# A TensorE order: gate, up, attention step, down of three units back, in place of gate, down of four units back, up, attention step

## What is computed

```
pooled = softmax(masked scores) @ x / count      # tanh scores, mask by prompt type
x1  = x + attention(pooled)                      # 16 heads of 8, low-rank keys and values, rotary part, causal
c   = x1 @ W[category of the sequence] + b       # one of 64 matrices for each sequence
x2  = x1 + sum over 64 experts of cw[token, e] * (silu(c @ Wg[e]) * (c @ Wu[e])) @ Wd[e]
         + shared expert, silu(c @ Wsg) * (c @ Wsu) @ Wsd
cw  = 8 of 64 experts for each token, chosen out of 4 of 8 groups, weights scaled by 2.5
```

## Time and profile before

| | us |
|---|---|
| median of 3 runs | 727.07 (725.82 to 727.83) |
| the profiled execution, its own time | 730.47 |
| span of its instructions | 728.6 |
| around the span | 1.87 |
| TensorE matmul busy | 704.1 (97% of the span) |
| VectorE busy | 543.2 (75%) |
| ScalarE busy | 444.0 (61%) |
| GpSimd busy | 424.5 (58%) |
| mean granted TensorE clock | 0.988 of full speed |

### The profile page before, as it was taken

How to read it: one execution, slowest core, us unless ns; L and a number is a source line. 1 busy time by engine, 2 the same in 40 slices (tenths; PEclk the granted TensorE clock), 3 DMA queues, 4 the chain that set the end, 5 groups by cost and what they waited for, 6 DMA issues and landing times.

```text
span 728.6 us, 15761 instructions
## 1 busy us (share of the span) xinstructions
PE 704.1 (97%) x5616; PEld 547.9 (75%) x5616; DVE 543.2 (75%) x1146; ACT 444.0 (61%) x857; POOL 424.5 (58%) x351
## 2 busy tenths in 40 slices
PE   7989889999999999999999999999999999999997
PEld 5767668677887778777787778877787777888885
DVE  4787568787598676887788865986768876877664
ACT  1876755568555865468555685558654685555553
POOL 2437677665456644556455654566455664666665
PEclk8998999999999999999999999999999999999999
DMA  7333674436443553534544364444544354344451
GB/s 257 107 113 124 202 149 112 124 104 163 106 124 114 145 109 121 138 101 146 120 112 137 107 157 105 126 113 140 113 125 138 97 150 115 110 129 142 128 130 46
DMA packets 66845, 92.93 MB, mean 128 GB/s; under 512 B 7888, under 2 KB 26768, under 8 KB 66768
## 3 DMA queue, kind: packets, MB, share of 16 engines
q1 hardware_dynamic: 61728, 85.90, 43.4%
q10 hardware_dynamic: 5040, 6.03, 2.5%
HBM read 88.37 MB, written 3.15 MB: 126 GB/s over the span
## 4 chain that ended last, share of the span: by engine, by line
PE 74%; DVE 10%; ACT 5%; SPq 4%; issue 4%; DMA 2%; POOL 1%; POOLq 0%; DVEq 0%; ACTq 0%
PE banks L997 71%; DVE hid L964 3%; DVE hid L976 2%; PE banks L1077 2%; DVE k_blk L693 1%; DVE pt_sb L668 1%; SPq L302 1%; ACT banks L531 1%; SPq L296 1%; DMA x_early<-in_x_feat 1%; SPq L272 1%; ACT s_t L405 1%; ACT hid_hi L543 1%; SPq L333 1%; ACT v_blk L392 1%
## 5 line engine op out<-in xcount | busy, mean ns | idle before, releaser
L640 POOL TENSOR_TENSOR hid_lo<-hid,hid_hi 128x512 fp32r<-128x512 f32 (+1 forms) x264 | 342.1, 1296 | 261.1 <-ACT hid_hi L543 259.3
L964 DVE TENSOR_TENSOR hid<-banks,cwb 128x512 f32<-128x512 f32 x254 | 174.6, 687 | 122.1 <-ACT banks L531 115.1
L531 ACT ACTIVATE banks<-banks 128x512 f32<-128x512 f32 x254 | 147.4, 582 | 134.3 <-PE banks L997 132.7
L543 ACT CAST hid_hi<-hid 128x512 fp32r<-128x512 f32 (+1 forms) x264 | 162.7, 616 | 78.7 <-DVE hid L976 76.9
L976 DVE TENSOR_TENSOR hid<-hid,banks 128x512 f32<-128x512 f32 (+1 forms) x264 | 181.4, 687 | 25.3 <-PE banks L997 2.9
L997 PE MATMUL banks<-c_hi,wg_hi 128*128 128x512 f32 x264 | 118.9, 450 | 4.6 <-DVE hid L964 3.4
L997 PE MATMUL banks<-hid_hi,wd_hi 128*128 128x512 f32 (+1 forms) x264 | 104.6, 396 | 0.8 <-POOL hid_lo L640 0.8
L997 PE MATMUL banks<-c_hi,wg_lo 128*128 128x512 f32 x264 | 104.0, 394 | 0.0
L997 PE MATMUL banks<-c_lo,wg_hi 128*128 128x512 f32 x264 | 104.0, 394 | 0.0
L997 PE MATMUL banks<-hid_hi,wd_lo 128*128 128x512 f32 (+1 forms) x264 | 103.7, 393 | 0.0
L997 PE MATMUL banks<-hid_lo,wd_hi 128*128 128x512 f32 (+1 forms) x264 | 103.6, 393 | 0.0
(11 more groups left out here) (159 smaller groups left out, 799.0 us busy)
## 6 DMA issues: line engine op xcount, KB each, us to landing
cwb<-cw_scratch SPq DMA_DIRECT2D x254, 256.0 KB, 3.8
k_blk<-in_cond_w SPq DMA_DIRECT2D x112, 64.0 KB
xf<-in_x_feat SPq DMA_DIRECT2D x8, 256.0 KB, 3.9
out_feat<-y ACTq DMA_DIRECT2D x8, 256.0 KB, 3.4
wg_raw<-in_we_gate SPq DMA_DIRECT2D x7, 256.0 KB, 4.7
wu_raw<-in_we_up SPq DMA_DIRECT2D x7, 256.0 KB, 4.5
wd_raw<-in_we_down SPq DMA_DIRECT2D x7, 256.0 KB, 4.5
xf<-in_x_tok SPq DMA_DIRECT2D x6, 256.0 KB, 2.7
```

The lines of the kernel that those rows point to most:

```text
L531: nc.scalar.activation(dst, gate_bank(p)[:, :], ACT.Silu).then_inc(S["silu_done"], 1)
L543: nc.scalar.copy(hid_hi[0:n, slot(b, p), :], hid[0:n, slot(b, p), :]).then_inc(S["hi_ready"], 1)
L640: nc.gpsimd.tensor_sub(hid_lo[0:n, slot(b, p), :], hid[0:n, slot(b, p), :], hid_hi[0:n, slot(b, p), :].bitcast(F32)).then_inc(S["lo_ready" ...
L964: nc.vector.tensor_mul(hid[:, slot(b, p), :], gate, weight)\
```

## The change

The order of the products on TensorE within a unit is another one; nothing else is touched. Before, unit p issues G(p), D(p - 4), U(p), A(p). After, it issues G(p), U(p), A(p), D(p - 3), and three D instead of four are left after the last unit. The row buffers stay at `NH` = 4, and the code of the other engines is the same. The operations and their number are the same too.

```diff
         Y_STORED = 4
+        BEHIND = 3
         X2_MOVED = 9
...
                 three(gate_bank(p)[:, :], wg_hi[:, p, :], wg_lo[:, p, :], c_hi[par][:, :], c_lo[par][:, :], True, True)\
                     .then_inc(S["gate_done"], 1)
-                if p >= NH:
-                    down(b, p - NH)
-                elif prev:
-                    down(b - 1, UNITS + p - NH)
                 if p < NPAIR:
...
                 for step, blk in steps:
                     attention_step(step, blk)
+                if p >= BEHIND:
+                    down(b, p - BEHIND)
+                elif prev:
+                    down(b - 1, UNITS + p - BEHIND)
 
             pe.sem_inc(S["y_ready"], 1)
             pipeline(unit)
-            for p in range(UNITS - NH, UNITS):
+            for p in range(UNITS - BEHIND, UNITS):
                 down(NBLK - 1, p)
```

## The result

| | before | after |
|---|---|---|
| median, us | 727.45 (725.82 to 727.87, 4 runs) | 740.37 (740.03 to 740.68, 4 runs) |
| profiled execution, its own time | 730.47 | 740.25 |
| its span | 728.6 | 738.4 |
| mean granted clock | 0.988 | 0.991 |

The changed kernel is slower: ratio 1.0173, 95% interval [1.0158, 1.0189], +12.6 us of 727.5. The medians are 12.9 apart and the forecast said 14.7. The two profiled executions are only 9.8 us apart, because the one of before began its block 0 late: first gate product at 45.96 us against 43.24, 2.7 of the missing 3.1 us, ahead of all that the change touches.

The account below looks back on a forecast made before the run. TensorE was taken to set the pace, so reordering could mainly lose time. Stalls of 4.1 + 4.1 + 0.4 + 2.5 + 2.9 + 0.7 = 14.7 us, added to the 727.07 median, gave 741.8 us; range 733.6 to 747.7.

Parts of the forecast that it names:

- A(7), A(8): Attention steps of units 7 and 8, blocks 1 to 6: no slack, full 0.69 us slip shows, 4.1 us.
- U(0), ends of blocks 0 to 5: Next block's first up product waits for hid(32) without slack: 6 x 0.69 = 4.1 us.
- U(0), end of block 6: First up product of block 7: slack 0.35, stall 0.34 plus 0.1 for a slow first matmul, 0.4 us.
- A(3): Attention step of unit 3, blocks 1 to 6: slack 0.25 or 0.30, stalls 0.44 and 0.39, 2.5 us.
- routing: Units 17 to 26: VectorE's stretch slips, stalls 0.47 or 0.12 plus 0.1 restart per block, 2.9 us.
- the end: Last down products wait for GpSimd's chain from the last gate product, one product later: 0.7 us.
- block 0: First block: waits on loading weights in units 8 to 13 absorb the slip; zero taken, up to 0.7 us possible.
- D had room: Down products one product earlier: even at the tightest place, in routing units, 0.39 of 1.77 us left; cost nothing.
- "faster" rival: Block 0: earlier down product fills a pause, keeping the clock from falling at 96 to 104 us; 724.7 us, chance 0.05.
- All hidden: Whole kernel: shorter waits before VectorE and ScalarE than shown take up the slip; 727 us, chance 0.08.
- part hidden: Only the unit 7/8 attention and block-end first up-product terms hold, 8.2 us: 735.3 us, chance 0.14.
- clock rival: Blocks 1 to 6: new pauses bring one low-clock stretch each, 10 us added; 752 us, chance 0.05.

Follow-up runs that it names:

- experiments 5 and 6: Kernel before, with gate products of only some units moved behind the down product (5; 28; 2; 17, 18; then 17-25; 28-32; 17-27): 730.06 to 732.64 us.
- experiment 3: Changed kernel with the gate product put back ahead of the down product in units 2, 4, 5, 17, 18 and 28: 727.11 us, ratio 0.9991.
- experiment 2: Kernel before with the attention step issued ahead of the up product in each unit: 751.21 us, ratio 1.0318.

## Why the prediction was right

The forecast, 741.8, is 1.4 us above the result (14.7 us added, 12.9 found), and its mechanism held at every place of blocks 1 to 7. By the starts of TensorE's matmuls (distance before and after; blocks 1, 3, 5, then 2, 4, 6):

| term of the sum | forecast | distances | measured |
|---|---|---|---|
| A(7), A(8) | 4.1 | A(7) 0.23 to 0.86 and 0.73; A(8) 0.64 unchanged, 0.49 to 0.63 | 6 x 0.63 or 0.64 = 3.8 |
| U(0), ends of blocks 0 to 5 | 4.1 | 0.43 to 1.13, 0.62 to 1.35 | 6 x 0.7 = 4.2 |
| U(0), end of block 6 | 0.4 | 0.23 to 0.42, and 0.33 for 0.23 behind it | 0.3 |
| A(3) | 2.5 | 0.32 to 0.75, 0.33 to 0.72 | 2.5 |
| routing | 2.9 | U(17) to U(28) +0.40, +0.21 | 1.8 |
| the end | 0.7 | U(31) to the end of the last matmul 6.27 to 7.09 | 0.8 |
| block 0 | 0 | first gate to that of block 1, with the slip | -0.9 |

The rows add up to 12.5 us. The two traces are 12.5 apart as well, counted from the first gate product to the end (9.8 by the spans and the 2.7 by which before began later), and the medians 12.9. (The last row: block 0 is 102.10 us long by its gates, 102.34 before. The next block's gate has slipped by 0.69, so by U and A block 0 is 0.93 shorter. This is no effect of the order that a run could show, see below; without it 13.4 of 14.7 us were found.) Of the 0.8 at the end 0.16 is the clock's: it was granted at 0.51 over the last 3.7 us, and the last matmul of all took 0.55 in place of 0.39.

*Right.* D had room: in blocks 1 to 7 no D but the last ones waits for its row. (In block 7 D(32) starts 0.32 behind U(2) and its next matmul 0.33 behind it, which looks like a pause. But its row is ready 2.50 us earlier, at 664.15 + 2.67 = 666.82 (the second of the two operations in that line), and the kernel before has the same two distances at its D(32): it is a product with 64 rows behind one with 128.) The first two lines are the kernel before, the others the changed one:

```profile
660.73 0.39 PE L997 MATMUL banks<-c_lo,wg_hi 128*128 128x512 f32 x1
661.04 0.49 PE L997 MATMUL banks<-hid_hi,wd_hi 64*128 64x512 f32 x1
...
664.15 2.67 POOL L641 TENSOR_TENSOR hid_lo<-hid,hid_hi 128x512 fp32r<-128x512 f32 x2 [0.80 <-ACT hid_hi L544]
...
669.00 0.39 PE L998 MATMUL banks<-c_lo,wu_hi 128*128 128x512 f32 x1
669.32 0.49 PE L998 MATMUL banks<-hid_hi,wd_hi 64*128 64x512 f32 x1
```

U and A kept their order and lost what their slack did not cover. The slack read at A(3), 0.25 and 0.30, was right within 0.02 us: a pause of 0.43 and 0.39 was measured for 0.44 and 0.39. A new detour of the chain appeared there. The places without slack passed on 0.63 (A(7) and A(8)) and 0.70 us (U(0)) of the slip of 0.69. The stalls did add up from place to place, which experiments 5 and 6 show one by one, and experiment 3 shows that nothing else adds to them in blocks 1 to 6.

*Routing mis-sized, 1.1 too high.* The step said: stall 0.47, and 0.1 for the restart, in blocks 0, 1, 3 and 5. In block 3 the delay at U(25), counted from U(17), is 0.46 (0.22 of it already at U(23), where TensorE pauses first), and a restart of 0.10 follows it, which is what the step said. But the kernel before already had a short pause at gate 26 (0.25 in place of 0.23, and a slow matmul behind it, 0.33 for 0.23), and this one went away: 0.56 - 0.12 = 0.44, with 0.40 left at U(28). I had counted a new cost and not the one that it replaces; that is 0.5 us over blocks 1, 3 and 5. The other 0.57 is block 0's, which no trace shows: the distance grew by 0.18 there, from 27.36 to 27.54 us, but in the kernels that have the old order up to unit 27 it is anything from 26.69 to 27.54, so 0.18 is no measure of the change. At gate 26 of block 3, before:

```profile
385.55 0.39 PE L997 MATMUL banks<-c_lo,wu_hi 128*128 128x512 f32 x1
385.80 0.50 PE L997 MATMUL banks<-c_hi,wg_hi 128*128 128x512 f32 x1
386.13 0.39 PE L997 MATMUL banks<-c_hi,wg_lo 128*128 128x512 f32 x1
```

*U(0) of block 7, 0.1 too high.* I took the start of hid(32) as set by the silu chain alone. The earlier trace rows shows what it was waiting for: 0.77 us, put down to TensorE. hid(32) was not held by its silu alone: it started 0.27 us behind G(0) (654.42 against 654.15), and in the changed kernel it starts 0.13 behind it (663.59 against 663.46). G(0) itself slipped by 0.69, so hid(32) slipped by 0.55, and the 0.35 of slack leave 0.20, for 0.19 measured. The code has the reason: VectorE waits for D(28) before hid(32) (L973). D(28) ended just ahead of hid(32), at 653.92 + 0.39 = 654.31; in the changed kernel it stands ahead of G(32), and hid(32) follows its silu (662.97 + 0.59 = 663.56). So the prediction's full slip at this place was a step too much: the start of hid(32) had a second wait, which the change relieves.

*Block 0.* The stretch from 96 to 104 us, at a clock of 0.79 in the earlier trace rows, has 8.00 us busy at 1.00 in the changed kernel. That is the piece of the "faster" rival that came true, some 1 us. Of the other eleven traces all but that of experiment 2 have such a stretch at the lower clock between 80 and 101 us, so the order may have a part in it, but no run separates this. I credit no gain to the order of the products: block 0 was 99.4 us long with gates 28 to 32 moved and 104.0 with gates 17 and 18 moved, though these two kernels have one order up to unit 16. Block 0 varies by more than the term.

*The rivals.* All hidden (727) and part hidden (735.3) are out by [1.0158, 1.0189]. The clock rival (752) did not come about: the clock was granted at 1.00 from 69.2 to 734.7 us, that is from block 0 to the last matmul. Its mechanism exists, as experiment 2 showed (that its 751.2 is near the 752 is chance, since most of its loss is pauses). The Trainium skill, in "TensorE: Matmul & The Clock Gate", section "A second HAM failure mode: psum-queue depth-cycling", tells of a kernel in which frequent short pauses between groups of matmuls made the clock go up and down. The changed kernel does not bear it out: it has half a dozen pauses of 0.1 to 1.1 us in each of blocks 1 to 6 with the clock at 1.00. In experiment 2 the clock did fall, each time behind a pause at A(3) that is longer than the one the change makes there.

## What to carry to other kernels

An in-order queue is read by slack: for each wait, how much earlier than needed is the result there, and at which instruction of this same queue did the chain to it start? Moving such a start by one product costs nothing in 27 of the 33 units of blocks 1 to 6 and the full 0.69 us in front of a wait that has no slack, so a reorder that looks uniform is a sum over a few places. The same reading says what to do instead: leave the heads of the chains alone, and move only ready work into the pauses that are there, which gave 0.88%.

When one head is moved, the instructions behind it that wait on the same engine must move as far, up to the end of that engine's unbroken stretch of work, or the next one that did not move pays a second time. That is what gates 23, 26 and 32 did in this kernel.

## What the runs showed of the hardware

- A pause costs more than its length. The first 512-column matmul behind one takes 0.50 us in place of 0.39, and the next one starts 0.33 to 0.34 us behind it in place of 0.23; this 0.10 us was paid behind pauses of 0.10 us as well as behind ones of 1.1. The same 0.50 and 0.34 stand, with no wait that the trace shows, behind the small matmuls of an attention step (G(1) of block 3 before: 321.81, then 322.15) and where products with 64 and 128 rows meet (D(32), above).
- TensorE starts 0.04 to 0.06 us after the end of the instruction that it waits for (hid ends at 320.73, the matmul starts at 320.77), at U(0), A(3), A(7) and the last D alike; at A(8) it is 0.14 (the copy of L353 ends at 342.06 in the kernel before, the transposes start at 342.19).
- The brackets of idle time leave out short pauses: those of 0.10 to 0.3 us have none, since the modelled end of the matmul before lies past them (387.43 + 0.39 = 387.82, with the next start at 387.76). The distance between starts shows them.
- The granted clock stayed at 1.00 with 1.8 us of pauses in a block of 86.6, and fell to 0.50 for 3.4 us after a pause of 1.1 to 1.2 us and 64 matmuls of 32 x 32 in five blocks of six (experiment 2); the sixth had the pause and not the fall.
